# Second attention of a hybrid block: row maxima handled four slots at a time, shifted scores eight slots behind the scores instead of eleven

## The reference, cut to what matters

```python
x = x + attn_a(layernorm(x))
x = x + ffn(layernorm(x))
x = x + attn_b(layernorm(x))     # the change lies here
x = x + ffn(layernorm(x))        # its routing begins while attn_b ends
```

## Time and profile before

| | |
|---|---|
| median of 3 runs | 1084.95 us (1084.47 to 1090.1) |
| profiled execution, its own time | 1086.67 us |
| its span, first to last instruction | 1084.9 us |
| mean granted TensorE clock | 0.867 of full speed |
| busy over the span | PE 971.3, DVE 959.2, ACT 671.2, POOL 368.7 us |
| second attention's slots, first maximum to last copy | 641.3 to 777.7 us |
| its end and the routing, to the last coefficients | 777.7 to 805.75 us |
| second pass of the experts | 807.17 us to the end |

### The profile page before, as it was taken

One profiled execution on the slowest core, in us unless ns is written; L12 is line 12 of the kernel. 1 busy time (PEld: TensorE's weight loads), 2 busy tenths in 40 slices (PEclk: granted clock), 3 DMA queues, 4 the chain that ended last, 5 costly groups with the idle time before them and its releaser, 6 DMA issues. The chain is left out here.

```text
span 1084.9 us, 17540 instructions
## 1 busy us (share of the span) xinstructions
PE 971.3 (90%) x5387; PEld 694.7 (64%) x5387; DVE 959.2 (88%) x1447; ACT 671.2 (62%) x848; POOL 368.7 (34%) x266
## 2 busy tenths in 40 slices
PE   6767887878669999999999899899889999999997
PEld 4533444444347888888888555455568888888886
DVE  7799999999988999999999797987589999999997
ACT  4779999999934545445445554876544544545544
POOL 2054666667901433333331211111203333333330
PEclk9865555555669999999999998999789999999999
DMA  2000000000119555555550000112049555555521
GB/s 59 1 1 1 1 1 1 1 1 1 52 30 215 157 160 151 147 157 147 155 153 4 1 1 1 23 23 31 16 107 225 151 147 157 148 154 155 147 85 39
DMA packets 50711, 86.94 MB, mean 80 GB/s; under 512 B 20092, under 2 KB 33404, under 8 KB 50556
## 3 DMA queue, kind: packets, MB, share of 16 engines
q1 hardware_dynamic: 50664, 86.34, 30.6%
HBM read 83.33 MB, written 2.98 MB: 80 GB/s over the span
## 5 line engine op out<-in xcount | busy, mean ns | idle before, releaser
L1514 ACT ACTIVATE sg<-ps 128x512 f32<-128x512 f32 x264 | 156.8, 594 | 264.8 <-PE ps L523 263.2
L523 PE MATMUL ps<-xh,whi 128*128 128x512 f32 x528 | 206.2, 391 | 1.3 <-ACT b L1330 1.3
L523 PE MATMUL ps<-xl,whi 128*128 128x512 f32 x528 | 205.9, 390 | 0.0
L523 PE MATMUL ps<-xh,wlo 128*128 128x512 f32 x528 | 205.8, 390 | 0.0
L2329 DVE TENSOR_TENSOR hf<-sg,ps 128x512 f32<-128x512 f32 x264 | 170.3, 684 | 29.9 <-DVE hl L2336 24.4
L1727 POOL CAST whi<-wraw 128x384 fp32r<-128x384 f32 x66 | 66.3, 1004 | 370.2 <-PE ps L523 285.5
L1647 POOL TENSOR_TENSOR rr<-xr,rr 128x2048 f32<-128x2048 f32 x32 | 145.2, 4569 | 125.0 <-ACT rr L1305 71.2
L2336 DVE TENSOR_TENSOR hl<-hf,hh 128x1024 fp32r<-128x1024 f32 x132 | 178.2, 1350 | 0.8 <-DVE hf L2329 0.8
L2341 DVE TENSOR_TENSOR hf<-hf,cbc 128x1024 f32<-128x1024 f32 x128 | 157.6, 1231 | 13.4
L1542 ACT ACTIVATE hh<-hf 128x1024 fp32r<-128x1024 f32 x132 | 139.2, 1055 | 4.6 <-DVE hf L2341 4.6
L1729 POOL TENSOR_TENSOR wlo<-wraw,whi 128x384 fp32r<-128x384 f32 x66 | 116.3, 1762 | 5.3
(11 more groups left out here) (277 smaller groups left out, 1512.3 us busy)
## 6 DMA issues: line engine op xcount, KB each, us to landing
cbc<-routing_coefficients SPq DMA_DIRECT2D x256, 256.0 KB, 3.8
wraw<-in_wexp_dram SPq DMA_DIRECT2D x66, 192.0 KB, 2.7
X<-in_x_dram SPq DMA_DIRECT2D x4, 256.0 KB, 4.8
routing_coefficients<-cT SPq DMA_DIRECT2D x8, 128.0 KB, 2.3
out_dram<-X SPq DMA_DIRECT2D x4, 256.0 KB, 2.9
heads_by_row<-o_all SPq DMA_DIRECT2D x12, 72.0 KB
b_rows<-heads_by_row SPq DMA_DIRECT2D x12, 72.0 KB, 2.7
rope_in<-in_consts_dram SPq DMA_DIRECT2D x1, 512.0 KB, 3.4
```

What stands on the lines that cost most here:

```text
L523: return pe.matmul(o, l, r, start=start, stop=stop, **kw)
L1514: act.activation(sg[c % 2][:, :], bank(4 + 2 * (c % 2)), ACT.Silu).then_inc(s_sg, 1)
```

## The change

1. The maxima are split, transposed, copied and spread for four slots (a quad, QUAD = 4, k = 0 to 15) in place of eight. Each step touches half the columns in the split (128x8 for 128x16); the transposes and ScalarE's copy keep their size and are done 16 times for 8. The number of spreads and shifts stays at 16. PE transposes at V % 4 == 1 (a slot later than before, seen from the last maximum it needs), and spreads at V % 4 == 2; VectorE shifts at V % 4 == 2.
2. AHEAD becomes 8: the prologue ends at V = 7, and after the last scores there are 11 passes for 14. Three fillers follow each of the prologue's slots V = 2 to 7.
3. The work of chunks 0 and 1 moves to V = 34, 35, 39, 40 (and 50, 51, 55, 56), with WAITS_FOR_PATH moved along.
4. The last 11 passes get 18 fillers (TAIL_FILL). The first half's routing rows are transposed at V = 59 and 63, their logits are computed at U = 56 and 57, and ScalarE copies them; the last two pairs of slots no longer wait for each other's copy, since one pair uses bank 2 (`pair_bank`).
5. VectorE's routing steps for the first half all run before the end of `last_of_b`, between the last chunk's steps; the second half's logits come before the last projection, and PE gets thirteen fillers there for ten (2, 2, 6, 3 for 3, 4, 3).
6. On GpSimd the bias addition stands behind the split of quad 3, and the normalisations behind those of quads 10 and 14.

```diff
-AHEAD = UNITS + 3
+QUAD = UNITS // 2
+AHEAD = QUAD + 4
+            n, at = ((0, 0), (1, 0), (1, 0), (1, 1))[2 * i + g]      # logit_bank, f == 1
+        def pair_bank(n):
+            return 2 if n == 2 * B - 2 else 6
-            WAITS_FOR_PATH = {39: 4, 46: 3, 47: 4, 55: 4, 62: 3, 63: 4}
+            WAITS_FOR_PATH = {36: 4, 41: 3, 42: 4, 52: 4, 57: 3, 58: 4}
+            TAIL_FILL = {56: 1, 57: 1, 58: 2, 59: 1, 60: 2, 61: 1, 62: 2, 63: 2, 64: 2, 65: 2, 66: 2}
...
-            def b_max_transposed(s):
-                pe.wait_ge(s_ms, s + 1)
+            def b_max_transposed(k):
+                pe.wait_ge(s_ms, k + 1)
...
+                k, at = V // QUAD - 1, V % QUAD
+                if 0 <= k < 2 * B:
+                    if at == 1:
+                        b_max_transposed(k)
+                    elif at == 2:
+                        b_max_selected(k)
...
                 for V in range(2, AHEAD):
                     b_tiles(-1, V)
                     b_max_step(V)
-                    if V >= AHEAD - 3:
-                        keep_busy(3, 6)
+                    keep_busy(3, 3)
...
-                if V in (38, 54):
+                if V in (35, 51):
...
-                elif V in (43, 59):
+                elif V in (39, 55):
...
+                elif V in (59, 63):
+                    pe.wait_ge(s_q2, V // QUAD)
+                    f_transposed(1, 0, (V - 59) // 4)
...
-                elif U == 59:
+                if U == 60:
                     pe.wait_ge(s_q2, 2 * B)
                     pe.wait_ge(s_on, B + 3)
                     transposed(2, 7)
...
+                keep_busy(6, 2)
+                pe.wait_ge(s_oTs, B + 3)
+                f_transposed(1, 1, 0)
+                keep_busy(6, 2)
                 pe.wait_ge(s_on, B + 5)
                 transposed(3, 2)
-                keep_busy(4, 3)
-                projected(3, 3)
-                f_transposed(1, 1, 0)
                 pe.wait_ge(s_ores, B + 3)
                 logits(1, 1, 0)
-                keep_busy(4, 4)
+                projected(3, 3)
+                keep_busy(4, 6)
                 f_transposed(1, 1, 1)
                 keep_busy(4, 3)
                 logits(1, 1, 1)
...
-                for s in range(B):
-                    max_split(s)
-                    if s == 1:
+                for k in range(2 * B):
+                    max_split(k)
+                    if k == 3:
                         pool.wait_ge(s_q2, 4)
                         pool.tensor_tensor(xb, xb, pb_s[:, :].unsqueeze(1).broadcast_to([P, TILES, P]), ALU.add
                                            ).then_inc(s_pbx, 1)
-                    elif s == 5:
-                        f_norm_apply_b(0)
-                f_norm_apply_b(1)
+                    elif k in (10, 14):
+                        f_norm_apply_b((k - 10) // 4)
...
-                    if at in (1, 2) and s >= 0:
-                        shift(s, at - 1)
-                    if V in (37, 53):
-                        normalise((V - 37) // 16)
+                    if V % QUAD == 2 and V > QUAD:
+                        shift(V // QUAD - 1)
+                    if V in (34, 50):
+                        normalise((V - 34) // 16)
...
+                x_low(1, 0, 0)
+                x_low(1, 0, 1)
+                shift(2 * B - 1)
                 marks(1)
+                sigmoids(1, 0, 0)
                 normalise(2)
-                sigmoids(1, 0)
+                sigmoids(1, 0, 1)
                 route_bests(1, 0)
-                route_groups(1, 0)
                 residual(2, 1)
                 stats_of(2)
+                route_groups(1, 0)
+                offset(2)
                 route_masks(1, 0)
                 normalise_last(0)
                 normalise_last(1)
-                offset(2)
+                route_masked(1)
                 residual(3, 3)
                 stats_of(3)
-                lows(1, 0)
+                route_marked(1)
                 offset(3)
+                route_weights(1, 0)
+                route_sums(1)
+                copy_xT(3, 6)
+                route_coefs(1, 0)
```

More of the change, by code:

```diff
@@ L929, in b_max_transposed, with b_max_selected @@
                 last.then_inc(s_mT, 1)
[L931 to L936, removed]
+            def b_max_selected(k):
+                pe.wait_ge(s_mr, k + 1)
                 for c in range(2):
-                    last = mm(bank(7)[:, c * N:(c + 1) * N], mxs[:, 2 * half + c, :], mxT[:, :])
+                    last = mm(bank(7)[:, c * N:(c + 1) * N], mxs[:, 2 * (k % 2) + c, :], mxT[:, :])
                 last.then_inc(s_mq, 1)
             def b_max_step(V):
[L943 to L947, removed]
+                k, at = V // QUAD - 1, V % QUAD
[4 more added lines that the diff above has]
+                        b_max_selected(k)
             def pv_b(C, half):
@@ L952, in pv_b @@
                 if C % 2 == 0 and half == 0 and C >= 2:
-                    pe.wait_ge(s_bev, C // 2)
-                last = pv(vt, s, c, wr[:, C % CHUNKS, :], bank(6)[:, C % 2 * N:(C % 2 + 1) * N], (half,))
+                    if pair_bank(C // 2) == 2:
+                        pe.wait_ge(s_mx, 2 * B * UNITS - 2)
+                    else:
+                        pe.wait_ge(s_bev, min(C // 2, 2 * B - 2))
+                last = pv(vt, s, c, wr[:, C % CHUNKS, :], bank(pair_bank(C // 2))[:, C % 2 * N:(C % 2 + 1) * N], (half,))
                 if half == MT - 1:
@@ L1429, in samples_b, with copy_xT, logit_exps @@
                         f_norm_rstd(1, 2)
[L1431 to L1432 removed]
+            def copy_xT(g, n):
+                act.wait_ge(s_fxnT, GROUPS + g + 1)
+                act.activation(f_xT[g][:, :], bank(n), ACT.Copy).then_inc(s_fxT, 1)
+                act.wait_ge(s_fxT, GROUPS + g + 1)
+                f_high(g)
+            def logit_exps(f, i, groups=range(2)):
+                act.wait_ge(s_lg, lap(f, i, groups[-1]))
                 if f == 0:
                     act.wait_ge(s_S, CHUNKS * B - 1)
[L1435 to L1436 removed]
+                for g in groups:
                     act.activation(route[f].sc[i][:, g * GTILES:(g + 1) * GTILES, :].rearrange("p t e -> p (t e)"),
[L1438 removed]
+                                   logit_bank(f, i, g), ACT.Exp, scale=-1.0).then_inc(s_sc, 1)
             def o_transposed_b(c, n):
@@ L2028, in prepare_f @@
                 if f == 1:
-                    route_experts(f, 0)
+                    lows(f, 1)
                 route_bests(f, 1)
@@ L2221, in head_max, with shift @@
                                           AX_X, ALU.max).then_inc(s_mx, 1)
-                def shift(s, half):
-                    dve.wait_ge(s_mq, 2 * s + half + 1)
+                def shift(k):
+                    s, half = k // 2, k % 2
+                    dve.wait_ge(s_mq, k + 1)
                     if s >= 2:
```

159 lines of the change are left out of this document (70 added, 89 removed).

## The result

The changed kernel took 1111.6 us (median of 4 runs, 1105.5 to 1113.2), the kernel before 1086.4 in the runs beside it: a ratio of 1.020 [1.017, 1.023]. The forecast was 1073.8. The profiled execution took 1112.6, 25.9 more than that of before; 25.65 of them lie ahead of the last coefficients.

The account below looks back on a forecast made before the run. Prediction: VectorE paces 681.4 to 751.1, PE the filled slots before; in the tail PE and ScalarE alternate at reduced clock. Gains 5.0 + 6.9 - 0.75 = 11.15 us off 1084.95 give 1073.8 us; range 1068 to 1081.5.

Parts of the forecast that it names:

- Slots 23 to 63: Second attention's quads: VectorE stays the pace at 5.46 us a quad, PE fits at 5.0; last maximum 5.0 us earlier.
- Filled slots: The twelve slots with two fillers each, set by PE: 20.1 us with the extra transposes and spreads, 19.1 before.
- A new wait: Before V = 22: quad 4's split waits behind GpSimd's 4.57 us bias addition; PE and VectorE stand, V = 22 1.8 us late.
- Rival D: Slower, 4 in 100: clock falls in the prologue, stays down through U = 11; filled slots lose 13 us, prologue 5: 1092.
- Prologue: Slots before the first shifted one: V = 8 to 10 and most of the wait go; V = 8 at 653.5, before 662.3.
- The split's five waits: VectorE's waits between 681.4 and 751.1 for PE behind GpSimd's split, some 0.7 us each, 3.4 in all, fall away.
- rival C: 11 in 100: ScalarE's extra copy delays PE and VectorE each quad, idle before each V % 4 == 3: 1077 to 1079.
- Tail: Last maximum to last copy, three passes fewer plus 18 fillers at full clock: 19.7 us instead of 26.6, gain 6.9.
- rival B: 20 in 100: the clock falls in the tail despite fillers; copy at about 27.5 instead of 19.7, total 1081.3.
- End: Last copy to last coefficients: 28.8 us against 28.05, so -0.75; early first-half routing gains nothing.

Follow-up runs that it names:

- run 1: The changed kernel with GpSimd's bias addition behind the split of quad 4 instead of quad 3: 1096.0 us, 1.006 of the kernel before.
- run 5: Run 1 with the shifted half nine slots behind instead of eight (odd distance): 1085.4 us, 0.9975 of the kernel before.
- run 6: The kernel before with the shifted half twelve slots behind instead of eleven (even distance): 1095.3 us, ratio 1.006.
- run 9: Run 1, still eight behind, with the shifted scores' two heads in the other order: 1087.8 us, 0.999 of the kernel before.
- run 4: Run 1 without the tail's 18 fillers (empty TAIL_FILL): 1090.7 us, 1.002 of the kernel before.
- run 7: Run 5 without the tail's fillers (empty TAIL_FILL): 1083.6 us, 0.996 of the kernel before.
- run 10: Run 9 without the tail's fillers (empty TAIL_FILL): 1087.1 us, 0.998 of the kernel before.
- run 3: The kernel before with its bias addition held back until the maxima of V = 21 are done: 1095.2 us, ratio 1.007.
- run 11: Run 10 with the end in the old order on TensorE and VectorE: 1084.1 us, 0.996 of the kernel before.
- run 12: Run 7 with the end in the old order on TensorE and VectorE: 1083.8 us, 0.996 of the kernel before.
- run 8: The changed kernel with nine slots behind, the bias addition left behind quad 3: 1090.2 us, 1.0015 of the kernel before.
- run 2: The changed kernel with eight fillers each ahead of V = 22 and V = 23, bias addition unmoved: 1100.7 us, 1.010 of the kernel before.

## Why the prediction was wrong

The forecast for the profiled execution was 1075.5 and it took 1112.6, 37.1 more: 4.75 of them lie ahead of V = 22, 27.0 between it and the last maximum, 5.2 in the tail and next to nothing behind. Two steps failed, the pace of PE and the price of the new wait.

**Slots 23 to 63** is the first. It took "a filled slot of 1.68 less the 0.7 of its fillers is 1.0" from the kernel before and set PE's quad at 5.0 us, under VectorE's 5.46. A slot of 1.0 is one in which the eight products take 0.45 us on four groups of rows. The change's even distance puts them on two, where they take 0.68 to 0.88, and the quad measured 6.26 in run 1. From V = 22 to the last maximum that made 77.1 us of 68.2, 8.9 too few in the sum. Runs 5, 6 and 9 show the cause from three sides; at the odd distance PE's plain slot is 1.01 us (689.33 to 690.34 in run 5), as forecast. I had read what the distance does to waits, and not which rows the neighbours in a slot then have.

**Filled slots** failed for the same reason: forecast 20.1, measured 21.9 in run 1 and 20.0 at the odd distance.

**A new wait** is the second. It was right in place, owner and length (PE 1.68 us, forecast 1.8) and wrong in price. I counted the stand alone. The clock fell behind it and stayed at 1.2 GHz for 51 us; V = 22 to the last maximum took 95.2 us against run 1's 77.1, so 18.1 us for that, the largest part of the miss. Rival D had a clock that falls and stays down, but in the prologue; there it was 1.00 from 646 on.

**Prologue**: V = 8 at 655.2 in the changed kernel and 653.9 in run 1, forecast 653.5. The clock, 0.73 over 640 to 646 in the changed kernel and 1.00 in run 1, makes the difference of the two. The split's five waits did fall away: VectorE's one wait a quad in run 1 comes from PE's length. **ScalarE's extra copy** (rival C) does not show where I put it, ahead of V % 4 == 3. But run 5's quad is 0.28 over VectorE's 5.46, and in it PE waits 0.23 us for ScalarE's copy of the outputs; whether the extra copy makes that one late was not tried.

**Tail**: 24.9 us (clock 0.86), 21.9 in run 1 at full clock, forecast 19.7. In run 1 the normalisation was done 11.3 us behind the last maximum (forecast 10.6), PE stood 1.90 (forecast 1.4), and each of the last three slots took 1.23 in place of 1.05. The clock fell in some profiles and held in others with the same fillers, so rival B is half right; and in all three pairs (runs 1 and 4, 5 and 7, 9 and 10) the kernel without the fillers had the shorter median, by 5.3, 1.8 and 0.7 us. They buy no time here, though only the first of these differences is clear of the spread.

**End**: 28.7 us, and 28.8 in run 1, forecast 28.8. The expert pass behind it took 279.4 us against 279.1 before; in run 1's profile it was 281.3. There the clock is at 0.51 from 1077.5 to 1081.0, near the end of the pass, and the profile of before has none of this. Of the fourteen profiles the nine with such a fall have 281.1 to 282.9 us for the pass, two kernels in the old arrangement (runs 3 and 6) among them, and the five without it 279.1 to 280.1. So the 2 us go with the clock, in the old arrangement as in the new one, and not with the change.

With both mistakes mended (run 5) a gain of 3.6 us is left, with an interval that reaches none, not 11. In its profile the last maximum ends at 751.7 (forecast 746.1): the first one starts 2.3 us later than in run 1 (643.5 and 641.2), the prologue is a slot longer, and the quad is 0.28 over VectorE's 5.46, ten times. The tail is 21.3. The late start is not the change's either: the clock is at 0.57 from 601 to 605, in code that no run touches, where it is at 1.00 in run 1, and that goes with most of the 2.3 us. Counted from the first maximum to the last coefficients, run 5 takes 157.6 us and the kernel before 164.4: 6.8 of the 11.15 came, and 4.7 were lost again in that start and in the expert pass (281.7). Three versions beat both kernels by some 5 us, runs 7, 11 and 12, at 0.996 of the kernel before; run 10 does by 1.9.

**Still open:** why the clock, once down, comes back within 3 to 7 us in runs 3 and 8 and stays down for 51 in the changed kernel. The arrangement of rows goes with it in these three, but whether the turned heads (run 9) with the stand would recover was not tried. And in run 6, an even distance, a fall at 713.4 was over at 716.8, behind four fillers, while four fillers at 717.8 did not end the one of the changed kernel.

## What to carry to other kernels

Where small products are packed on groups of rows, the distance between two interleaved streams also decides which rows they use beside each other: write down the rows of every pair of neighbours before changing it, and keep them apart by parity, or, if that can't be had, spread each burst over both groups by turning one stream over. Before a long instruction is put ahead of a short one on an engine that feeds TensorE, count not only the stand but what may run at half clock behind it. Where two causes may meet, vary both: the square of four runs gave 15.6 us or 4.8 for the same stand, by what stood around it. And look at the clock in the stretches that the change leaves alone before a difference of 2 us is put down to the change.

## What the runs showed of the hardware

A stand of PE of 1.68 to 2.00 us for GpSimd's split was followed by a fall of the clock in all four kernels that had one (the changed kernel, runs 2, 3 and 8), and where the split came in time there was none at that place. But a stand as long does not always bring a fall. For the normalised rows of chunk 0 PE stood 1.84 us in run 5 and 2.69 in run 7, and the clock held; it stood 1.96 in run 8 and 2.69 in run 12, and the clock fell. Run 5:

```profile
701.40 0.63 PE L1008 MATMUL ps<-cst,b_otok 128*128 128x128 f32 x4 [1.84 <-DVE b_otok L2249]
```

```profile
702.00:705.00 3.00, 3.00 (x37) 1.68 (x35) 2.03 (x4) 1.49 (x4) 0.70 (x4) 1.00 0.00 0
```

Stands of 1.86 to 1.90 in the tail were followed by a fall in the changed kernel and in run 9, and not in run 1. The Trainium skill ("TensorE: Matmul & The Clock Gate", "Why this matters for your kernels") warns of longer idle gaps than these; here shorter ones were enough in some places and not in others.

Once low, the clock stayed at 0.50 through 40 us in which PE was busy for 39.8 (688 to 728, changed kernel). A busy PE alone did not bring it back, and four fillers of 2.06 us in this stretch did not either; it came back at the end of a projection of 2.08 us. In run 2 it was back by the end of eight fillers of 3.37 us, and in runs 3 and 8 with no filler at all.

Eight products of 32 rows took 0.44 to 0.45 us on four groups of rows (before and run 5). On two groups they took 0.66 to 0.68 at best, in either order of the heads. With all four products of a head on the same rows they took 0.77 to 0.88 in other slots, of which some 0.2 us is ScalarE's copy in one slot of four; with the heads turned (run 9) such slots were gone.
